# A two-layer selective-scan stack on one core: pair-wide scan inputs, five of sixteen states summed by ScalarE and GpSimd, the skip term by TensorE

## The reference

```python
xc, z = jnp.split(x @ W_in.T, 2)                # 2 x 1024 channels
u = silu(conv4(xc) + b_c)                       # depthwise, 4 taps, causal
dt, B, C = jnp.split(u @ W_x.T, [32, 48])       # 32 + 16 + 16
delta = softplus(dt @ W_dt.T + b_dt)
h[d, n] = exp(delta[d] * A[d, n]) * h[d, n] + delta[d] * B[n] * u[d]   # over t, 16 states n
y[d] = sum_n(h[d, n] * C[n]) + u[d] * Dp[d]
out = (y * silu(z)) @ W_out.T
```

## Time and profile before

| | us |
|---|---|
| median of three runs (lowest to highest) | 9130.06 (9126.48 to 9130.49) |
| the profiled execution, first to last instruction | 9119.7 |
| what lies around that span: median less span | 10.4 |
| first scan starts / last scan of the two layers starts | 241.3 / 8262.5 |
| one chunk, from `c_now` copy to `c_now` copy, mean of 30 | 251.2 |
| DVE busy of the span | 8449.9 (93%) |
| PE, POOL, ACT busy of the span | 7422.6, 6002.9, 5597.6 |

### The profile page before, as it was taken

How to read it: one execution, slowest core, us unless ns; L and a number is a source line. 1 busy time by engine, 2 the same in 40 slices (tenths; PEclk the granted TensorE clock), 3 DMA queues, 4 the chain that set the end, 5 groups by cost and what they waited for, 6 DMA issues and landing times. The chain is left out here.

```text
span 9119.7 us, 124311 instructions
## 1 busy us (share of the span) xinstructions
PE 7422.6 (81%) x29640; PEld 3968.2 (44%) x29640; DVE 8449.9 (93%) x9986; ACT 5597.6 (61%) x9722; POOL 6002.9 (66%) x4680
## 2 busy tenths in 40 slices
PE   5788888888888888888888888888888888867886
PEld 3444444444444444444444444444444444444753
DVE  2999999999999999999999999999999999996716
ACT  5666666666666666666666666666666666643515
POOL 0777777777777777777777777777777777772203
PEclk7899999999999999999999999999999999968888
DMA  5111111111111111111111111111111111113434
GB/s 191 43 48 47 47 41 48 48 48 44 48 48 47 46 47 43 46 59 58 57 45 48 48 48 47 47 47 44 49 48 49 45 49 49 44 41 119 184 118 147
DMA packets 221783, 552.86 MB, mean 61 GB/s; under 512 B 24496, under 2 KB 24752, under 8 KB 200048
## 3 DMA queue, kind: packets, MB, share of 16 engines
q1 hardware_dynamic: 194672, 459.30, 15.8%
q10 hardware_dynamic: 26368, 84.95, 2.3%
HBM read 442.44 MB, written 101.71 MB: 60 GB/s over the span
## 5 line engine op out<-in xcount | busy, mean ns | idle before, releaser
L769 POOL TENSOR_TENSOR bu<-w,b_rep 128x512 f32<-128x512 f32 x4096 | 5210.2, 1276 | 2178.9 <-DVE h L804 2171.6
L804 DVE TENSOR_TENSOR_SCAN h<-decay,h_last,bu 128x512 f32<-128x512 f32 x3840 | 4882.7, 1272 | 28.5 <-POOL bu L769 19.9
L644 ACT ACTIVATE decay<-delta,neg_a 128x512 f32<-128x512 f32 x4096 | 2802.9, 689 | 2839.7 <-DVE h L804 2822.1
L438 PE MATMUL turn<-ident_m,h 128*128 128x128 f32 x16384 | 2698.5, 290 | 1321.7 <-DVE h L804 726.7
L438 PEld LDWEIGHTS turn<-ident_m,h 128*128 128x128 f32 x16384 | 1984.6, 147 | 3918.2 <-issue 2041.9
L815 DVE SCALAR_TENSOR_TENSOR acc<-turn,c_now,acc 128x512 f32<-128x512 f32 x3840 | 2777.3, 723 | 5.3 <-PE turn L438 4.0
L382 PE MATMUL proj<-x_conv,w_in 128*128 128x512 f32 x2048 | 1088.1, 624 | 54.7 <-issue 29.2
L382 PE MATMUL proj<-zy,w_out 128*128 128x512 f32 x2048 | 1050.0, 607 | 2.5 <-issue 2.5
L382 PE MATMUL proj<-conv_in,conv_diag 128*128 128x512 f32 x2048 | 1040.1, 602 | 9.6 <-ACT halo L561 9.6
L382 PE MATMUL proj<-x_gate,w_in 128*128 128x512 f32 x2048 | 1023.1, 594 | 0.0
L804 DVE TENSOR_TENSOR_SCAN h<-decay,zeros_m,bu 128x512 f32<-128x512 f32 x256 | 325.3, 1272 | 125.2 <-POOL bu L769 125.1
(11 more groups left out here) (167 smaller groups left out, 5480.4 us busy)
## 6 DMA issues: line engine op xcount, KB each, us to landing
b_rep<-b_rows SPq DMA_DIRECT2D x1024, 256.0 KB, 3.2
x_conv<-xt SPq DMA_DIRECT2D x32, 1024.0 KB, 6.2
x_gate<-xt SPq DMA_DIRECT2D x32, 1024.0 KB, 6.4
xt<-stage ACTq DMA_DIRECT2D x128, 256.0 KB, 2.4
x_n<-in_x_dram SPq DMA_DIRECT2D x16, 1024.0 KB, 5.2
xt<-xt_n ACTq DMA_DIRECT2D x16, 1024.0 KB, 4.1
x_l<-in_x_dram SPq DMA_DIRECT2D x16, 1024.0 KB, 5.7
mt_l<-xt SPq DMA_DIRECT2D x16, 1024.0 KB, 5.4
```

The costliest lines, as they stand in the source:

```text
L438: mm = pe.transpose(turn[:, tn.n % RING, b * P:(b + 1) * P], h[:, k % 2, b, j * P:(j + 1) * P], ident[:])
L644: act.activation(decay[:, b, :], delta[:, blk, :], ACT.Exp, scale=neg_a[:, n, blk:blk + 1]).then_inc(decay_set, 1)
L769: pool.tensor_tensor(bu[:, b, :], w[:, blk, :], b_rep[:, k % 4, :], ALU.mult).then_inc(bu_set, 1)
L804: dve.tensor_tensor_scan(h[:, k % 2, b, :], decay[:, b, :], bu[:, b, :], start, ALU.mult, ALU.add).then_inc(scanned, 1)
```

## The change

Six edits, all inside the two Mamba layers. `decay` stays in its four PSUM banks as before.

1. `bu` has four buffers of two blocks. POOL makes the input of two slots in one 128x1024 instruction (`inputs`, L857), with `b_rep` broadcast over the two blocks, and may run up to 8 slots ahead instead of 4. The softplus sum and product are 128x1024 as well (L839, L846), and sit where `W_AT` puts them.
2. States 2, 5, 8, 11 and 13 of each half: ACT multiplies the turned bank by C into `prod` (L690, 40 in a chunk), POOL adds two of them at a time to `acc` (L865, 20 in a chunk). DVE has no `add_state` for these states.
3. The skip term: `d_diag` holds diag(D), PE multiplies `u` with it into a `turn` bank (4 matmuls of 128x128 for each of 8 tiles), ACT copies that into `acc` (L697), and the first state is added on top. `ud` and `sum_y` are gone; `gate_y` reads the `turn` bank from PSUM.
4. The bias of `delta` comes in as row 64 of `w_dt`, against a row of ones in `xdbl`.
5. Exp and Ln of softplus are 128x1024, and `exp_tables` loads one table set for both after each Silu.
6. `ORDER` is written out with earliest slots; ACT takes a tile 4 slots after PE has filled it. PE turns group `k - 1` in group `k` (its own list was numbered 4 slots earlier before).

```diff
-DELTA_W_AT = tuple(range(8, 16))
-DELTA_W_NEXT_AT = tuple(range(24, GROUPS))
+RATE = 1.4
+TAKE_LAG, TAPS_LEAD, W_LAG, X_PROJ_LAG, XDBL_LAG, CONV_LAG, PROD_LAG = 4, 2, 10, 5, 3, 4, 3
+            for q, part in enumerate(("sum", "product")):
+                w_at[(end + W_LAG) // 2 + q].append((part + kind[5:], x // 2))
+BY_ACT = (2, 5, 8, 11, 13)
+Y0_AT = (80, 82, 84, 86)
+Y1_AT = (6, 8, 10, 12)
+SKIP_AT = (0, 15)
+TURNS = 2
...
-    bu = sb("bu", [P, 4, T])
+    bu = sb("bu", [P, 4, 2, T])
+    prod = sb("prod", [P, J, HB * P])
...
+        def product(G, kind, k, j):
+            tile = "state", k, j
+            act.wait_ge(turn_full, turn_base(G, kind) + (kind.turns.index[tile] + 1))
...
+            if j % 2 == 0:
+                act.wait_ge(vsum_set, G * ADDS_ALL + (ADDS[k] + j // 2 - 1 + C_PROD))
+            act.activation(prod[:, j, :], turn[:, kind.turns.index[tile] % TURNS, :], ACT.Copy,
+                           scale=c_now[:, j, k % STATES:k % STATES + 1]).then_inc(v_done, 1)
...
+                    k_now, j = divmod(s - PROD_LAG, J)
+                    if k_now - 1 in ADDS:
+                        product(G, kind, k_now - 1, j)
...
-            pool.wait_ge(scanned, G * SCANS + (4 * k + b + 1))
-            pool.tensor_tensor(bu[:, b, :], w[:, blk, :], b_rep[:, k % 4, :], ALU.mult).then_inc(bu_set, 1)
+            pool.wait_ge(scanned, G * SLOTS_BODY + (s - 6 + C_SCAN))
+            pool.tensor_tensor(bu[:, s // 2 % 4, :, :], w[:, blk:blk + 2, :],
+                               b_rep[:, k % 4, :].unsqueeze(1).to_broadcast([P, 2, T]), ALU.mult).then_inc(bu_set, 1)
+
+        def add_products(G, kind, k, jp):
+            lo = 2 * jp
+            pool.wait_ge(v_done, G * V_TILES + (kind.turns.by_act["state", k, lo + 1] + 1 + C_PROD))
...
+            pool.tensor_tensor(acc[:, k // STATES, lo:lo + 2, :], acc[:, k // STATES, lo:lo + 2, :], prod[:, lo:lo + 2, :],
+                               ALU.add).then_inc(vsum_set, 1)
...
+                k, pr = divmod(p, 2)
+                inputs(G, k, pr)
+                if k - 2 in ADDS:
+                    add_products(G, kind, k - 2, pr)
...
+            elif k - 1 in ADDS:
+                dve.wait_ge(vsum_set, G * ADDS_ALL + (ADDS[k - 1] + j // 2 + 1 + C_PROD))
...
-            dve.tensor_tensor(zy[:, b, :], ud[:, b, :], zy[:, b, :], ALU.mult).then_inc(y_set, 1)
+            dve.tensor_tensor(zy[:, blk, :], turn[:, i % TURNS, :], zy[:, blk, :], ALU.mult).then_inc(x_done, 1)
```

More of the change, by code:

```diff
@@ L89, in timetable @@
 def timetable():
[L92 to L104, removed]
+    at, end_of = 0.0, {}
@@ new lines, in timetable, with tiles @@
+        if kind == "conv" and x % HB == HB - 1:
+            take[end + TAKE_LAG].append(("silu_u", x // HB, i))
+        if kind == "gate" and x % HB == HB - 1:
+            take[end + TAKE_LAG].append(("silu_z", x // HB, i))
+    return work, take, w_at, end_of
+WORK, TAKE, W_AT, END_OF = timetable()
+def tiles(first, last):
+    kept = [i for i, (kind, _, _) in enumerate(ORDER) if not (first and kind in NOT_FIRST or last and kind in NOT_LAST)]
+    return {i: n for n, i in enumerate(kept)}, len(kept)
@@ new lines, with by_act, __init__ @@
+TURN_AT = turn_tiles()
+CARRIED = [("state", GROUPS - 1, j) for j in range(J)] + [("y", 1, b) for b in range(HB)]
+def by_act(tile):
+    return tile[0] == "skip" or tile[0] == "state" and tile[1] % STATES in BY_ACT
+class Turns:
+    def __init__(self, order):
+        self.order = order
+        self.index = {t: i for i, t in enumerate(self.order)}
+        self.by_dve, self.by_act, dve, act = {}, {}, 0, 0
+        for t in self.order:
+            self.by_dve[t], self.by_act[t] = dve, act
+            if by_act(t):
+                act += 1
+            else:
+                dve += 1
+        self.n_dve, self.n_act = dve, act
@@ L154, in __init__, with has @@
         self.layer_next = layer + self.leaves
+        self.place, self.n_tiles = tiles(self.first, self.last)
+        self.turns = FIRST_TURNS if self.first else END_TURNS if over else ALL_TURNS
+    def has(self, what):
+        return not (self.first and what in NOT_FIRST or self.last and what in NOT_LAST)
 def all_chunks(eng, run):
@@ new lines, in turn_y, with turn_tile @@
+        def turn_y(out, summed, hf, b):
+            pe.wait_ge(x_done, summed)
+            for j in range(J):
+                mm = pe.transpose(out[:, j * P:(j + 1) * P], acc[:, hf, j, b * P:(b + 1) * P], ident[:])
+            mm.then_inc(turn_full, 1)
+        def turn_tile(G, kind, tile):
+            what, x, j = tile
+            out = turn_bank(G, kind, tile)
+            if what == "skip":
+                skip(out, G, kind.layer, x, j)
+            if what == "state":
+                turn_states(out, G - (tile in CARRIED), x, j)
+            if what == "y":
+                last = "state", x * STATES + STATES - 1, J - 1
+                turn_y(out, dve_base(G, kind) + (kind.turns.by_dve[last] + 1 + C_TURN), x, j)
@@ new lines, in body @@
+        def body(G, kind):
+            for s in range(SLOTS_BODY):
+                k, j = divmod(s, J)
+                if s == J:
+                    turn_now(G, kind)
+                scan(G, kind, k, j)
+                for tile in TURN_AT[s]:
+                    what, x, at = tile
+                    if tile in kind.turns.index and what == "state" and x not in ADDS:
+                        add_state(G, kind, x, at)
+                    if tile in kind.turns.index and what == "y":
+                        gate_y(G, kind, tile)
@@ L872 @@
+        all_chunks(dve, body)
+        for tile in CARRIED:
+            if tile[0] == "state":
+                add_state(G_END, Kind(LAYERS - 1, over=True), tile[1], tile[2])
+            else:
+                gate_y(G_END, Kind(LAYERS - 1, over=True), tile)
 LOWEST = -3.4e38
```

743 lines of the change are left out of this document (381 added, 362 removed).

## The result

The changed kernel takes **9190.55 us** (median, 9189.51 to 9193.40), the kernel before 9130.27 in the same rounds: ratio 1.0068, 95% interval 1.0054 to 1.0082. It is 0.7% slower, where a faster kernel and 8713 were forecast. The forecast's chunk was 238.2 us; thirty chunks now take 8110.64 - 491.95 = 7618.7 us, 254.0 each, against 251.2 before. These 15.8 us a chunk are 473 of the 477 us of error. So the chunk's account is the place to look.

The account below looks back on a forecast made before the run. DVE was taken to bound the kernel. Its 215.8 us plus 22.4 of stalls made a 238.2 us chunk, 13.0 less; 30 chunks and the ends saved 417 us, giving 8713 us, range 8530 to 8910.

Parts of the forecast that it names:

- DVE's own work: DVE's instructions in one chunk after the change, without stalls: scans, 88 adds, gates, `c_now` and loop, 215.8 us.
- POOL's 2.31 a step: Each wide POOL instruction in a chunk steps on by 2.31 us; 92 of them make 212.5 us, against 182 before.
- ACT's 178: ACT's work in a chunk after products and skip copies come in: 178 us of 238, costed at nothing.
- gates and inputs without extra cost: Gates at 0.61 us, free of the POOL lock with one PSUM input; broadcast `b_rep` inputs at 2.31 us.
- POOL's sums make DVE wait with group 29 as the worst: DVE stalls for product states' sums 22.4 us a chunk; 8.3 for second-half state 11, with four softplus instructions in group 29.
- 7 and 13: First-half groups where DVE's third add waits for the second sum of states 5 and 11: 3.7 us each.
- 10: First-half group where DVE waits for state 8's second sum, held up by ACT's products: 0.8 us.
- Rival 1: POOL's sums come early enough and DVE stays the bound: 215.8 us a chunk, 8020 us in all; chance 0.06.
- PE: 8 skip tiles of 0.43 us, with 100 us of slack: Skip-term tiles added to PE in each chunk, listed among the edits costed at nothing.
- 144 large matmuls: PE's large matmuls in a chunk before, about 0.43 us each; with 137 tiles about 121 us, not 208 busy.
- Rival 3: ACT's products hold both `turn` banks, stalling PE, then DVE: 262.7 us a chunk, 9500 in all; chance 0.10.
- 1.3 us for the loop: DVE's remainder in a measured 251.0 us chunk beyond its 249.6 us of instructions, kept in the 215.8 us after.

## Why the prediction was wrong

**Right.** DVE's own work (215.8 forecast, 214.5 measured), POOL's 2.31 a step, ACT's 178, gates and inputs without extra cost, and that POOL's sums make DVE wait with group 29 as the worst. Not so group by group: 7 and 13 lose 0.6 and 0.5 where 3.7 each were forecast, and 10 loses 2.9 where 0.8 was; I read this as POOL catching up while DVE waits for PE, which no run tested. Rival 1 (no waits) falls with the 40 us.

**The step that failed** is "PE: 8 skip tiles of 0.43 us, with 100 us of slack". It failed in three ways.

1. *The size.* "144 large matmuls" at "about 0.43 for each" came from the earlier trace rows, whose x4 counts records. They are two matmuls. The 288 records of a chunk are 124 us, the 136 turned tiles 58, the 8 skip tiles (8 records, 0.86 us each, not 0.43) 7: 189 us of work in a chunk and not 121. A slot of a bare scan (1.19 us) asks PE for a tile and 1.4 matmuls, 1.63 us; with a skip tile it is 2.5. The Trainium skill, "FP8 and Floating Point Precision", TensorE Precision Notes, says that a true FP32 matmul makes four passes. The Trainium skill, "TensorE: Matmul & The Clock Gate", "Wait — 56ns, not 53.3ns?", gives 215.7 ns from one matmul of 512 columns to the next at full clock, so an estimate by these pages is 0.86. The trace agrees: 2 records take 1.02 us and 4 take 1.88, 0.86 for one matmul more. Counting it so would have more than halved the slack.
2. *The wait that I didn't list.* DVE's bare scans run ahead of PE by design, and the second group after them needs PE's last tile because `h` has two buffers. Before, DVE waited for turned tiles 49 us in the whole span; now 564 (314.0 + 249.6). Rival 3 named the two banks that ACT's products hold and priced them by ACT's stalls. Its mechanism, PE in order behind ACT, is a part of the true one (group 3's rows), its price was far too high (9500), and 0.10 was too low a chance.
3. *The chunk's end.* The change moves state 31's tiles of PE behind the loop's jump and its other work before group 27. Groups 31 and 0 lose 10.5 us a chunk, 1.8 of it for POOL's sum. The forecast had 1.3 us for the loop, on DVE alone, and nothing for PE, though group 1's longer time after it (11.6 against 8.6 us in layer 1) stood in the trace of before.

**The range** took in POOL's unknowns and not PE's, since the busy row of PE (208 us a chunk) was argued away by the mistaken size. The account in the looped chunks, which says who released DVE and not yet why PE was late: PE +21.2, "issue" +2.1, other small waits +1.6, POOL's part 7.2 less than forecast, DVE's own work 1.3 less: +16.4, beside 15.8 over all thirty.

## What to carry to other kernels

When work leaves the bound engine in bursts (four bare scans here), the other in-order engines have to keep up within the burst, not over the chunk: add up each one's work slot by slot there, and name the buffer that ties it to the burst. Moving an add to two slower engines paid in this kernel for five states placed where POOL's work between two due sums fits DVE's time: with half of the jumps and spread skip tiles they made the kernel 3% faster (0.9699, 0.9683 to 0.9715), 229 us of it by the states themselves, where the change with ten packed ones was 0.7% slower. Which states pay has to be tried: two more cost 125 us. Before calling an engine's busy share overstated, count its records against the instructions in the code.

## What was not expected of the hardware

- A 128x512 float32 matmul is two records of 0.43 us, a 128x128 one two of 0.11; a transpose of 128x128 is one of 0.11.
- At a hardware loop's jump in these long bodies DVE stands 2.8 to 4.0 us in the changed kernel and 0.7 to 1.0 in the kernel before. PE's idle stretch there is 3.7 to 5.4 us in layer 1 of the changed kernel and 6.9 to 11.0 in layer 2, 2.8 of it before the scan that its tile waits for has ended. Unrolling by two gave 39 us in the kernel before and 105 in the changed one.
- The granted clock is 0.5 when PE starts the new chunk, whether it was so before (changed kernel) or fell in the idle time (1.00 to 0.50 with tiles turned three times), and the first tiles take about twice as long as at 2.4 GHz (1.11 against 0.60).
- A `to_broadcast` input costs GpSimd nothing: 2361 ns against 2358 for the sum of the same size without it.
